# Shared network on one core: the copy of the 64 odd inner rows' values, one step further back in ScalarE's order

## What is computed

```python
resonance = jnp.einsum('bli,hi->blh', x, basis)          # 32 harmonics
w = amp * jnp.cos(phase); q, k, v, o = einsum('blh,oh->blo', resonance, w)
attn = softmax(q @ k.T * head_dim ** -0.5)               # 16 heads of 16
y = silu(x @ wg[e]) * (x @ wu[e]) @ wd[e]                # 8 experts, the best 2 of each token, 352 inner rows
shared = silu(x @ sw_gate) * (x @ sw_up) @ sw_down       # 704 inner rows
```

## Time and profile before

| | us |
|---|---|
| median of 3 runs | 1026.63 (1023.13 to 1027.21) |
| the profiled execution, whole | 1023.98 |
| its span, first to last instruction | 1022.2 |
| TensorE busy | 943.7 (92%) |
| VectorE busy | 642.1 (63%) |
| ScalarE busy | 567.0 (55%) |
| GpSimd busy | 310.3 (30%) |
| mean granted clock of TensorE | 0.958 of full |

### The profile page before, as it was taken

One profiled execution on the slowest core, in us unless ns is written; L12 is line 12 of the kernel. 1 busy time (PEld: TensorE's weight loads), 2 busy tenths in 40 slices (PEclk: granted clock), 3 DMA queues, 4 the chain that ended last, 5 costly groups with the idle time before them and its releaser, 6 DMA issues.

```text
span 1022.2 us, 17669 instructions
## 1 busy us (share of the span) xinstructions
PE 943.7 (92%) x5627; PEld 634.4 (62%) x5628; DVE 642.1 (63%) x979; ACT 567.0 (55%) x892; POOL 310.3 (30%) x297
## 2 busy tenths in 40 slices
PE   5965899999999978899999999999999999999998
PEld 4945799999999963345545545545545545545546
DVE  7677833444433446666686686686686686786753
ACT  5556544444444444556566566566566666666563
POOL 1003222222222206125135135135135235135232
PEclk9975899999999985889999999999999999999999
DMA  9897155222222235445555555555555555534220
GB/s 308 329 286 265 49 143 169 68 67 77 67 72 72 68 94 150 129 113 143 181 135 139 183 136 143 174 143 140 179 138 144 177 134 146 177 96 100 61 63 21
DMA packets 94032, 139.91 MB, mean 137 GB/s; under 512 B 18153, under 2 KB 51441, under 8 KB 92945
## 3 DMA queue, kind: packets, MB, share of 16 engines
q1 hardware_dynamic: 87280, 121.25, 41.1%
q0 software_dynamic: 6480, 17.70, 5.9%
q10 hardware_dynamic: 208, 0.14, 0.0%
HBM read 79.63 MB, written 54.71 MB: 131 GB/s over the span
## 4 chain that ended last, share of the span: by engine, by line
PE 67%; DVE 9%; issue 8%; ACT 7%; SPq 4%; DMA 2%; POOL 2%; ACTq 0%; POOLq 0%
PE bank L1307 9%; PE bank L1213 8%; PE st_pair L1318 7%; PE s_pair L1195 7%; PE bank L1373 7%; PE st_pair L1195 7%; PE bank L1330 6%; PE s_pair L1269 5%; ACT prob L1002 5%; DVE top L1701 4%; PE bank L1100 3%; PE bank L1203 2%; DVE h_f L1725 2%; PE bank L1178 1%; DMA q_rows<-top_T 1%
## 5 line engine op out<-in xcount | busy, mean ns | idle before, releaser
L1701 DVE TENSOR_REDUCE top<-s_pair 128x2 f32<-128x1024 f32 x252 | 308.6, 1225 | 148.9 <-PE s_pair L1269 147.8
L1002 ACT ACTIVATE prob<-st_pair 128x1024 f32<-128x1024 f32 x256 | 260.7, 1018 | 175.2 <-PE st_pair L1318 172.1
L750 POOL TENSOR_TENSOR h_T<-h_f,h_T 128x512 fp32r<-128x512 f32 x40 | 51.4, 1285 | 363.6 <-ACT h_T L984 363.6
L728 POOL DMA_INDIRECT xg<-xn_rows,token_of x71 | 69.8, 984 | 276.5 <-PE bank L1178 188.7
L1318 PEld LDWEIGHTS st_pair<-q_rows,k_rows 50*128 50x128 f32 x512 | 48.7, 186 | 168.8 <-ACT prob L1002 124.3
L1318 PE MATMUL st_pair<-q_rows,k_rows 50*128 50x512 f32 x512 | 130.5, 505 | 18.2 <-ACT prob L1002 10.5
L1307 PE MATMUL bank<-xT_b,w_sh 128*128 128x512 f32 x528 | 146.0, 412 | 0.0
L1330 PE MATMUL bank<-prob,v_ones 128*32 128x512 f32 x1024 | 139.0, 615 | 0.0
L1269 PE MATMUL s_pair<-k_rows,q_rows 48*128 48x512 f32 x504 | 113.0, 441 | 6.3 <-DVE top L1701 5.6
L1307 PEld LDWEIGHTS bank<-xT_b,w_sh 128*128 128x128 f32 x528 | 94.2, 191 | 31.6 <-issue 12.2
L1213 PE MATMUL bank<-w_exp,c_hT 128*128 (+1 forms) x639 | 93.6, 291 | 1.0 <-ACT c_y L930 1.0
(11 more groups left out here) (224 smaller groups left out, 1184.2 us busy)
## 6 DMA issues: line engine op xcount, KB each, us to landing
qk_rows<-qk_hi SPq DMA_DIRECT2D x56, 256.0 KB
q_rows<-qk_rows SPq DMA_DIRECT2D x64, 192.0 KB
k_rows<-qk_rows SPq DMA_DIRECT2D x56, 192.0 KB
expert_rows<-c_y SPq DMA_DIRECT2D x71, 128.0 KB, 1.7
xn_T_split<-x_T SPq DMA_DIRECT2D x8, 1024.0 KB, 5.1
xT_b<-xn_T_split SPq DMA_DIRECT2D x32, 256.0 KB, 4.6
qk_rows<-qk_lo SPq DMA_DIRECT2D x28, 256.0 KB
x_all<-in_L_attn_x_dram SPq DMA_DIRECT2D x8, 512.0 KB, 8.3
```

The costliest lines, as they stand in the source:

```text
L728: pool.indirect_dma_start(xg[s % 4][:, :], None, xn_dram, bass.IndirectOffsetOnAxis(token_of[:, s:s + 1], 0)).then_inc(c_x[s % 4], 16)
L750: pool.tensor_tensor(h_T[0:m, LO, f, :], h_f[q % 2][0:m, :], h_T[0:m, HI, f, :].bitcast(F32), ALU.subtract).then_inc(p_h, 1)
L1002: act.activation(prob[kt % 2][:, 2 * jp:2 * jp + 2, :].rearrange("p j l -> p (j l)"), st_pair[:, :], ACT.Exp, scale=HD ** -0.5).then_inc(a ...
L1701: dve.tensor_reduce(top[g % 2][:, :, jp, qt], score_pair(b, g, v)[:, :].rearrange("p (i k) -> p i k", i=2), AX_X, ALU.max).then_inc(d_max, 1)
```

## The change

ScalarE's copy of the 64 odd rows' values (`hidden_high` for the tile `BOTH`) is issued two steps after the tile's gate product instead of one. A new function `unit_two` gives the unit of two steps before. The copy thus moves from step 6 of group 1 to step 7, where it stands behind the exponent of step 7, the group's last. The copies of the other tiles stay where they were. No other engine's list is changed.

```diff
--- before.py
+++ after.py
@@ -385,6 +385,9 @@
 
         def unit_before(b, g, t):
             return unit(b, g, t - 1) if t else unit(*after(b, g, -1), STEPS - 1)
+
+        def unit_two(b, g, t):
+            return (b, g, t - 2) if t >= 2 else after(b, g, -1) + (STEPS - 2 + t,)
 
         def of(b):
 
@@ -1045,8 +1048,11 @@
                         ao_high(ppb, ppg // 2)
                     if (b, g, t) == (LAST, 3, 7):
                         last_o_high(0)
+                    what, c, i = unit(*unit_two(b, g, t)) if t else (None, None, None)
+                    if what == "gate" and i == BOTH:
+                        hidden_high(c, i)
                     what, c, i = unit_before(b, g, t)
-                    if what == "up" or what == "gate" and i == BOTH:
+                    if what == "up":
                         hidden_high(c, i)
                     if what == "out":
                         low_rank_o_high(c)
```

## The result

The changed kernel takes 1018.55 us in the median of 20 runs (1013.9 to 1022.21), the kernel before, measured with it, 1024.8 us (20 runs, 1019.06 to 1027.44). The ratio is 0.9945 with a 95% interval of 0.9929 to 0.9962: 5.6 us faster (3.9 to 7.3), where 6.05 us were forecast. That the kernel is faster is clear; that it is faster by over the 0.5% (5.1 us) named in the prediction is not, since the interval reaches from 0.38% to 0.71%. The profiled execution took 1019.23 us with a span of 1017.4 us, 4.8 us less than that of before.

The account below looks back on a forecast made before the run. TensorE, busy 92%, bounds the kernel and waits for step 7's exponent, held behind ScalarE's copy. Rounds 1 to 7 give 3.15 us, round 0 2.9 us: 6.05 us off 1026.63 gives 1020.6 us, range 1016.5 to 1025.0.

Parts of the forecast that it names:

- (1): Step 7 of group 1: the exponent starts 0.60 us after its scores, at 512.48 instead of 513.92 in round 1.
- (2): The moved copy starts behind that exponent, at about 513.45 in round 1; VectorE's maximum covers it, so it costs nothing.
- (3): TensorE's transposed scores of step 0 of group 2 come 0.88 us earlier, the upper bound for a round.
- (4): VectorE's maximum, low part, maximum are late next, leaving 0.45 us gain in each of rounds 1 to 7.
- Step (5): Round 0: TensorE's hole is split and the clock stays at 2.4 GHz, gaining 2.9 us; 0.95 us if it falls.
- A: The forecast itself, with the clock staying up in round 0: gain 6.05 us, 1020.6 us; chance 0.60.
- B: Round 0's remaining holes still lower the clock, or it falls in both kernels: gain 4.1 us, 1022.5 us; chance 0.20.
- the small places: Elsewhere in the rounds, not priced by the prediction; three are weight loads of L1318 waiting for the maxima's transfer.
- Rival C: Another wait closes in, the maxima's transfer or late next-round loads: gain 0 to 2 us, about 1025.5 us; chance 0.15.
- Rival D: The copy ends too late and VectorE's low part waits for it: 6 us slower, 1032.6 us; chance 0.05.

Follow-up runs that it names:

- kernel with the low part later: Changed kernel with VectorE's low part of the odd rows moved from step 7 of group 1 to step 2 of group 2; ratio 0.9934 to the kernel before.
- the filled hole: Six extra TensorE products, into a bank nothing reads, in round 0's step 7 of group 1; ratio 0.9942 in the changed kernel, 0.9974 in the kernel before.
- kernel one step further back: Changed kernel with the copy moved behind the exponent of step 0 of group 2, the low part left in step 7; ratio 1.0149 to the kernel before.
- low part later, loads moved: Changed kernel with the low part in step 2 of group 2 and SP's q_rows and k_rows loads ahead of half of xT_b; ratio 0.9940.

## Why the prediction was right, point by point

**Steps (1) and (2)**, the exponent and the copy: right to a few hundredths. Exponent 0.60 us behind the scores forecast, 0.54 found; the copy starts at the end of the exponent's overlap, exactly with VectorE's maximum, as at the lower end given; the price of nothing for it was tested by doubling it.

**Steps (3) and (4)**, the bound of 0.88 us and VectorE as the next to be late: right. The scores of step 0 came 0.95 us earlier (3.18 - 2.23), 0.07 us beyond the bound, since they start 0.08 us before the recorded end of the six output products and not behind it. Forecast 0.45 us a round, found 7.49 - 7.05 = 0.44 us in round 1 and 0.42 to 0.55 in the others. The wait for the maximum before the score pair, forecast at 0.1 to 0.4 us, is on record with 0.37 before the weight load at 513.43. The kernel with the low part later shows that this instruction held 0.18 us of the 0.5 us that was lost between the 0.95 us and the 0.44 us; that the two maxima and the pair between them hold the rest is read from the timeline and was not tested.

**Step (5)**, round 0: the 2.9 us were right for an execution in which the clock stays up (6.79 us of passage against 6.83 forecast, seen four times), but too much as a term that counts in every execution. Round 0 in all profiles without the filled hole, but for the kernel one step further back:

| kernel | passage of round 0, us | to step 7 of group 2, us | clock after it |
|---|---|---|---|
| before | 9.75 | 20.34 | down |
| moved in rounds 1 to 7 alone | 8.60 | 19.18 | down |
| before, second profile | 10.04 | 20.62 | down |
| changed | 8.34 | 19.96 | down |
| changed, second profile | 7.97 | 18.55 | down |
| changed, third profile | 6.77 | 17.77 | up |
| moved in round 0 alone | 6.79 | 17.38 | up |
| copy twice | 6.78 | 18.15 | up |
| low part later | 9.37 | 20.31 | down |
| low part later, loads moved | 6.63 | 17.52 | up |

With the copy unmoved in round 0 the clock fell in three profiles of three, with the copy moved in three of seven. So few profiles, on three chips, do not show that the move makes the fall less frequent; they show that with it the fall can fail to come. The kernel one step further back adds to this: TensorE waits 0.97, 0.57 and 1.16 us in its round 0, more than in the changed kernel, and the clock stayed up. From step 7 to step 7, the mean of the three unmoved is 20.05 us and that of the five moved ones with VectorE's order unchanged 18.36 us: 1.7 us on average instead of 2.9. Part of the shortfall is the fall that still comes, part the rows that are late when it doesn't (17.77 and 18.15 against 17.38). What rivals A and B describe is both found: the changed kernel itself has the fall in two profiles and not in the third. With the copy unmoved the fall came 2.3, 4.5 and 3.0 us after the scores of step 7; this agrees with the Trainium skill (TensorE: Matmul & The Clock Gate, "What's actually happening"), by which the watch over TensorE isn't tied to a kernel's start. With the 0.4 us of the small places, a term that the prediction put at nothing, the sum becomes 3.1 + 1.7 + 0.4 = 5.2 us, and 5.6 us (3.9 to 7.3) were measured. The interval holds the 4.1 us of rival B too, so the measured time doesn't tell the two sums apart. So the failed part of step (5) is its frequency: the sum counted a thing that comes in some executions as one that comes in all.

**Rival C** was named in two forms. The transfer of the maxima did not close in on rounds 1 to 7. In round 0 the weight load at 434.21 has it as its recorded releaser, while the exponent that it needs as well ends at 434.10, so it costs 0.1 us at most; the load stands 3.09 us behind the issue at 431.12, where the prediction took 2.78 us, and that it cost so little is in part luck. The late load for the next round did: in three of the profiles where the clock stayed up, by 1.0 to 1.9 us (weight load's wait). The forecast had put it into a rival of its own; it belongs to A, since only A is fast enough to meet it.

**Rival D** did not happen, and happened on request: one step more and the kernel is 16 us slower.

The forecast of 1020.6 us for a median of 1018.55 leans on a "before" of 1026.63 us from three runs; with 20 runs it is 1024.8 us, and 6.05 us less than that is 1018.75 us. That the number came within 0.2 us of this is luck in part, since step (5) was too high by 1.2 us on average and the small places were left out. The gain is what was forecast within its interval.

## What to carry to other kernels

Where engines take their work in the order written, look for an instruction that waits for another engine and has urgent work queued behind it; put it behind that work, but only as far as its own consumer is covered by something else, and read that cover off the timeline (here a maximum that ran 0.6 us longer than the copy; one step further made the kernel 16 us slower than before). Then price what is late next before counting the stall as gain: 0.89 us of waiting gave 0.44. Where a hole in TensorE's work is cut, look at the granted clock behind it, count its return only as a chance, and check the loads for the next stage, which were timed for the slower pace.

## What the runs showed of the hardware that was not expected

Additional work on TensorE made the kernel faster (six products more, 2.7 us less), since it kept the clock up over a hole. A hole of 2.45 us brought the clock down in all three profiles that have it, and the holes of 1.7 us in the kernel one step further back were followed by a fall in each of rounds 1 to 7, while the 0.89 us before the scores of step 0 in rounds 1 to 7 of the kernel before never did.

On the second and third chip every kernel, that of before included, took 50 us more (1078.63 and 1079.5 us for the kernel before). The changed kernel's second profile shows the reason by stretches: once in each round TensorE, VectorE and ScalarE all stand still for some 5 us, here from 489 to 494 us, and the clock falls behind it. The exponent and the maximum then start in the same hundredth of a microsecond; the profile names no engine or transfer of this core as the releaser.

```profile
480.00:489.00 9.00, 8.83 (x62) 5.79 (x64) 4.42 (x5) 4.58 (x7) 7.04 (x7) 1.00 0.85 216
489.00:494.00 5.00, 0.92 (x8) 0.01 (x3) 0.26 (x1) 0.25 (x1) 1.89 (x2) 1.00 0.73 221
494.00:501.00 7.00, 6.17 (x25) 4.80 (x25) 3.14 (x6) 2.39 (x3) 0.00 (x0) 0.56 0.23 80
```

```profile
493.74 1.23 DVE L1707 TENSOR_REDUCE top<-s_pair 128x2 f32<-128x1024 f32 x1 [7.50 <-remote]
493.75 1.02 ACT L1005 ACTIVATE prob<-st_pair 128x1024 f32<-128x1024 f32 x1 [6.21 <-remote]
```

The profiles on the first chip have no such stop. What it is stays open; it lies outside the passage, and the two ratios of the changed kernel agree (0.9945 and 0.9938).
